# Layers: the second pair of q/k products of a half visit moved between the output turns and the output product

## The reference

```
def attn_layer(x, Wqkv, qs, ksc, Wo):
    q, k, v = split(x @ Wqkv, 3)                   # 16 heads of 64
    q = l2norm(q) * qs
    k = l2norm(k) * ksc
    q = q * cos * scale + rotate_half(q) * sin * scale
    k = k * cos / scale + rotate_half(k) * sin / scale
    out = local_attention(q, k, v)                 # windows of 32, softmax
    return out @ Wo
for i in range(6):
    x = attn_layer(shift_tokens(x), ...) + x
    x = ffn_layer(shift_tokens(x), ...) + x
```

## Time and profile before

| | us |
|---|---|
| median of 3 runs | 4645.14 (4640.55 to 4652.28) |
| profiled execution, own time | 4643.52 |
| its span, first to last instruction | 4641.7 |
| TensorE busy | 4093.0 (88%) |
| VectorE busy | 3365.0 (72%) |
| ScalarE busy | 2392.2 (52%) |
| GpSimd busy | 2163.8 (47%) |

### The profile page before, as it was taken

One profiled execution on the slowest core, in us unless ns is written; L12 is line 12 of the kernel. 1 busy time (PEld: TensorE's weight loads), 2 busy tenths in 40 slices (PEclk: granted clock), 3 DMA queues, 4 the chain that ended last, 5 costly groups with the idle time before them and its releaser, 6 DMA issues. The chain is left out here.

```text
span 4641.7 us, 175927 instructions
## 1 busy us (share of the span) xinstructions
PE 4093.0 (88%) x68914; PEld 2806.2 (60%) x68915; DVE 3365.0 (72%) x7216; ACT 2392.2 (52%) x5386; POOL 2163.8 (47%) x2301
## 2 busy tenths in 40 slices
PE   7999749576999889998899989999889998899995
PEld 4566416454666656666566665666656666566663
DVE  4777450576888778887788877888778887788876
ACT  4666423123666546665366653666536665366651
POOL 2444300103566436664366643666436664366651
PEclk9999769798999999999999999999999999999998
DMA  1000003003333223332233322333223332223221
GB/s 41 5 5 3 1 21 98 8 0 85 66 71 66 47 65 70 66 68 49 65 70 64 71 48 65 67 67 69 50 65 66 68 68 51 64 64 71 62 57 43
DMA packets 478517, 249.52 MB, mean 54 GB/s; under 512 B 65782, under 2 KB 472516, under 8 KB 476740
## 3 DMA queue, kind: packets, MB, share of 16 engines
q1 hardware_dynamic: 477764, 238.93, 23.1%
HBM read 35.40 MB, written 4.19 MB: 9 GB/s over the span
## 5 line engine op out<-in xcount | busy, mean ns | idle before, releaser
L1921 POOL TENSOR_TENSOR n_pre<-n_tt 128x512 f32<-128x512 f32 x768 | 970.9, 1275 | 886.1 <-DVE n_tt L2394 886.1
L2394 DVE TENSOR_TENSOR n_tt<-n_pp,n_rot 128x1024 f32<-128x1024 f32 x768 | 922.2, 1220 | 378.6 <-ACT n_sq L2255 378.5
L1942 POOL TENSOR_TENSOR n_pre<-n_pre,n_rn 128x512 f32<-128x512 f32 x768 | 776.6, 1042 | 284.4 <-ACT n_rn L2263 284.4
L2021 PE MATMUL n_pp<-n_wqkv,n_xT 128*128 128x512 f32 x1536 | 787.9, 615 | 10.7 <-ACT n_xT L2250 10.4
L2255 ACT ACTIVATE n_sq<-n_pp 128x512 f32<-128x512 f32 x768 | 459.1, 598 | 595.5 <-PE n_pp L2021 584.7
L2401 DVE TENSOR_REDUCE n_ss<-n_sq 128x8 f32<-128x512 f32 x768 | 518.8, 676 | 0.0
L2275 ACT COPY n_qkT<-n_pp 128x512 f32<-128x512 f32 x768 | 436.6, 594 | 136.6 <-PE n_pp L2037 136.1
L2037 PE MATMUL n_pp<-ident,n_pre 128*128 128x128 f32 x3072 | 433.2, 274 | 19.7 <-POOL n_pre L1942 14.5
L2051 PE MATMUL n_pp<-n_wo,n_OT 128*128 128x128 f32 x3072 | 398.7, 283 | 58.1 <-ACT n_OT L2281 57.1
L2037 PEld LDWEIGHTS n_pp<-ident,n_pre 128*128 128x128 f32 x3072 | 360.3, 142 | 129.1 <-issue 125.4
L2051 PEld LDWEIGHTS n_pp<-n_wo,n_OT 128*128 128x128 f32 x3072 | 361.4, 193 | 103.6 <-ACT n_OT L2281 101.2
(11 more groups left out here) (246 smaller groups left out, 7016.9 us busy)
## 6 DMA issues: line engine op xcount, KB each, us to landing
n_V<-n_Vn SPq DMA_DIRECT2D x768, 128.0 KB, 2.6
n_Vx<-n_Vn SPq DMA_DIRECT2D x384, 128.0 KB, 2.5
n_Vx<-n_Vn SPq DMA_DIRECT2D x576, 64.0 KB, 2.2
n_wqkv<-in_L_ffn_Wqkv SPq DMA_DIRECT2D x6, 1536.0 KB, 6.7
e_w<-in_L_ffn_w SPq DMA_DIRECT2D x32, 256.0 KB, 3.0
n_fxs<-X SPq DMA_DIRECT2D x48, 127.0 KB
m_Y<-e_ye SPq DMA_DIRECT2D x64, 64.0 KB, 2.1
n_wo<-in_L_ffn_Wo SPq DMA_DIRECT2D x6, 512.0 KB, 7.3
```

Source lines behind the costliest of these rows:

```text
L1921: nc.gpsimd.tensor_tensor(d, s[0], s[1][:, :, ::-1, :], ALU.add).then_inc(s_add, 1)
L1942: nc.gpsimd.tensor_tensor(d, d, bcast(rn[:, j, t, 8 * half:8 * half + 8], 2, D), ALU.mult).then_inc(s_kn, 1)
L2021: nc.tensor.matmul(pp[:, c % 2, :], xT[:, j * P:(j + 1) * P], wqkv[:, t * I + 512 * half:t * I + 512 * half + 512], start=True, stop=True) ...
L2394: nc.vector.tensor_tensor(tt[:, c % 4, :, :].rearrange("p s (h d) -> p s h d", d=D), bcast(pp[:, c % 2, :].rearrange("p (h d) -> p h d", d ...
```

## The change

In each half visit the second pair of q/k products (c = 4j+2 and 4j+3) is issued between the output turns and the output product; before, one stood behind the second turn of q/k and the other at the end of the half. The two first turns of q/k now stand together, ahead of the turns of the weights. On ScalarE the two squares follow the copies of the output and stand ahead of the exponentials. On VectorE the two rotations follow the maxima and the sum of squares 4j+1, ahead of the sums of the exponentials; the addition of the output product to X comes behind these sums, and the two sums of squares come last. `sq` has four buffers in place of two, and a square waits for the sum four before it, in place of two.

```
--- before.py
+++ after.py
@@ -1717,7 +1717,7 @@
         eye = sb("eye", [P, P], BF16)
         xs = sb("xs", [P, 2, NT, C])
         xT = sb("xT", [P, T + 1])
-        sq = sb("sq", [P, 2, 512])
+        sq = sb("sq", [P, 4, 512])
         tt = sb("tt", [P, 4, 2, 512])
         ss = sb("ss", [P, NT, 2, H])
         rn = sb("rn", [P, NT, 2, H])
@@ -2155,23 +2155,21 @@
                     elif prev:
                         turn_output(N - 1, 2, bank("o", 2, -1))
                         turn_output(N - 1, 3, bank("o", 3, -1))
+                    if nxt:
+                        project_qk(N + 1, 4 * j + 2)
+                        project_qk(N + 1, 4 * j + 3)
                     if prev:
                         output(N - 1, j, bank("y", j, -1))
                     d = j
                     if nxt or not d:
                         turn_qk(N + d, 4 - 4 * j, bank("turn", 4 - 4 * j, d))
+                        turn_qk(N + d, 5 - 4 * j, bank("turn", 5 - 4 * j, d))
                     turn_weights(N, j)
-                    if nxt or not d:
-                        turn_qk(N + d, 5 - 4 * j, bank("turn", 5 - 4 * j, d))
-                    if nxt:
-                        project_qk(N + 1, 4 * j + 2)
                     if nxt or not d:
                         turn_qk(N + d, 6 - 4 * j, bank("turn", 6 - 4 * j, d))
                         turn_qk(N + d, 7 - 4 * j, bank("turn", 7 - 4 * j, d))
                     if j == 1 and nxt2:
                         turn_x(N + 2, u, bank("x", 0, 2))
-                    if nxt:
-                        project_qk(N + 1, 4 * j + 3)
                 if not nxt:
                     weights_ready(pairs[0], N, u, 1)
                     held(pe, s_held)
@@ -2250,9 +2248,9 @@
                 nc.scalar.copy(xT[64:P, 1:T + 1], pp[64:P, bank, 0:T]).then_inc(s_xT, 1)
 
             def square(N, c):
-                after(act, s_ss, 8 * N + c - 1)
+                after(act, s_ss, 8 * N + c - 3)
                 after(act, s_qk, 8 * N + c + 1)
-                nc.scalar.activation(sq[:, c % 2, :], pp[:, c % 2, :], ACT.Square).then_inc(s_sq, 1)
+                nc.scalar.activation(sq[:, c % 4, :], pp[:, c % 2, :], ACT.Square).then_inc(s_sq, 1)
 
             def inverse_norms(N, j):
 
@@ -2326,21 +2324,19 @@
                     elif prev:
                         copy_output(N - 1, 2, bank("o", 2, -1))
                         copy_output(N - 1, 3, bank("o", 3, -1))
+                    if nxt:
+                        square(N + 1, 4 * j + 2)
+                        square(N + 1, 4 * j + 3)
                     exps(N, j, 0)
                     exps(N, j, 1)
                     if nxt or not j:
                         copy_qk(N + j, 4 - 4 * j, bank("turn", 4 - 4 * j, j))
+                        copy_qk(N + j, 5 - 4 * j, bank("turn", 5 - 4 * j, j))
                     copy_weights(N, j, 0)
                     copy_weights(N, j, 1)
                     if nxt or not j:
-                        copy_qk(N + j, 5 - 4 * j, bank("turn", 5 - 4 * j, j))
-                    if nxt:
-                        square(N + 1, 4 * j + 2)
-                    if nxt or not j:
                         copy_qk(N + j, 6 - 4 * j, bank("turn", 6 - 4 * j, j))
                         copy_qk(N + j, 7 - 4 * j, bank("turn", 7 - 4 * j, j))
-                    if nxt:
-                        square(N + 1, 4 * j + 3)
                 if nxt2:
                     copy_x(N + 2, bank("x", 0, 2))
                 if not nxt:
@@ -2399,7 +2395,7 @@
                 j, t, half = place(c)
                 after(dve, s_rn, 2 * N + j - 1)
                 nc.vector.tensor_reduce(ss[:, j, t, 8 * half:8 * half + 8],
-                                        sq[:, c % 2, :].rearrange("p (h d) -> p h d", d=D), AX.X, ALU.add
+                                        sq[:, c % 4, :].rearrange("p (h d) -> p h d", d=D), AX.X, ALU.add
                                         ).then_inc(s_ss, 1)
 
             def maxima(N, j):
@@ -2456,13 +2452,14 @@
                     maxima(N, j)
                     if nxt:
                         sum_squares(N + 1, 4 * j + 1)
+                        rotate(N + 1, 4 * j + 2)
+                        rotate(N + 1, 4 * j + 3)
+                    sum_exps(N, j)
                     if prev:
                         add_attention(N - 1, b - 1, j, at["y", j, -1][0])
-                    sum_exps(N, j)
                     if nxt:
-                        for c in (4 * j + 2, 4 * j + 3):
-                            rotate(N + 1, c)
-                            sum_squares(N + 1, c)
+                        sum_squares(N + 1, 4 * j + 2)
+                        sum_squares(N + 1, 4 * j + 3)
                     if not nxt and not j:
                         stats(layer[0] * NG, 0)
                         normalise(layer[0] * NG, 0)
```

2 lines of the change are left out of this document (removed).

## The result

| | before | changed |
|---|---|---|
| median, us | 4647.47 (4640.55 to 4652.28, 4 runs) | 5092.31 (5077.87 to 5098.34, 4 runs) |
| profiled execution, us | 4643.52 | 5092.21 |
| mean granted clock of TensorE | 0.961 | 0.944 |
| TensorE busy, us | 4093.0 (88%) | 4189.6 (82%) |

The ratio is 1.0954, 95% interval 1.0926 to 1.0981: slower by 9.5%. The forecast was 5065, range 4930 to 5175.

A forecast was written before the change was run, and what follows sets the result against it. TensorE was taken to set the pace, standing still for VectorE's late addition. On the profiled 4643.5 us, 328 for the stalls gave 4971, and 94 for the clock gave 5065; range 4930 to 5175.

The forecast's parts named there:

- The bank: TensorE's second turn of q/k waits for its PSUM bank until VectorE's late addition to X: 2.4 us per half.
- T+7.3: Predicted end of VectorE's addition with its signal, 7.3 us after the half's output turns start (T); turn due at T+4.92.
- The stall per element: Masks come 2.0 and 1.9 us later in the two halves: 3.9 us per element, 84 elements, 328 us.
- ScalarE's late exponentials: Exponentials behind the squares run 1.3 us later on ScalarE; claimed free, as VectorE reaches their sums later still.
- From masks to output turns: Program unchanged in this stretch; priced at nothing, staying 6.98 us where the clock is 1.00.
- The first and last elements: Per layer, the first can gain 13 us in all, the last lose 9.4; between these bounds nothing was taken.
- the bound of 13: Most the first elements could gain: their 2.17 us wait for the exponentials, once a layer, 13 us.
- The clock: TensorE's clock falls to half behind some stalls, costing 2.8 us per element: 84 x 0.4 x 2.8 = 94 us.
- Two in five: Share of the new TensorE stalls followed by half clock, taken from 5 of 12 similar waits in the trace.
- The Trainium skill's rule: Cycling PSUM banks with short TensorE idle times swings the clock between half and full; in full, it gives 5206.
- the rival that took it in full: Every stall is followed by the half clock: 235 us, 5206; chance 0.14, shared with more than three in five.
- that term from minus 40 to nothing: TensorE's 40.1 us of instruction waits in the product with V could vanish while it stands: 4931 at the lowest.

The follow-up runs named there:

- e1: The changed kernel with VectorE's addition of the output product to X moved between the two rotations: 4656.98 us, ratio 1.0022 to before.
- e4: The changed kernel with the addition to X also behind VectorE's two sums of squares: 5396.40 us, ratio 1.1604.
- e6: The changed kernel with the exponentials ahead of the two squares again on ScalarE: 5256.64 us, ratio 1.1311.
- e2: The changed kernel with the turns of the weights again between the first two turns of q/k, addition still late: 4908.38 us, ratio 1.0566.
- e10: As e9, but second q/k product behind the second turn of q/k, and turns of the weights between the first two turns: 4580.71 us, ratio 0.9868.
- e9: Kernel before with only product 4j+2 moved early, 4j+3 behind the last q/k turn, first two turns together, addition ahead of rotation 4j+2: 4543.25 us, ratio 0.9789.
- e3: The changed kernel with the edits of both e1 and e2: 4685.82 us, ratio 1.0087.
- e7: e1 with TensorE's two bursts of small matmuls (product with V, scores) cut in halves, large products between: 4686.53 us, ratio 1.0075.
- e8: The kernel before with the same cut of the two bursts as e7 and nothing else: 4738.45 us, ratio 1.0192.

## Why the prediction was right

**The bank.** The wait that cost nothing in the earlier trace rows is the one that decides. It was predicted at T+7.3 and came at T+7.14: the reciprocal lets the addition follow after 0.17, not after its whole 0.25, and the addition took 0.23, not 0.29. e1 takes that wait away, but for 0.2 us, and all but 10 us of the loss go with it; e4 and e6 lengthen it and the loss grows with it.

**The stall per element.** A clean half of the changed kernel takes 16.51 us, one with the turn of x 17.31 (from one second turn of q/k to the next); before, 14.59 and 15.43. That is 3.8 us per element, predicted 3.9: 84 x 3.8 = 319 us, predicted 328.

**What was priced at nothing.** ScalarE's late exponentials cost nothing, as said (e1, e6). From masks to output turns a clean half takes 7.00 against 6.98, as said. The first and last elements do not show in sum: the wait for the exponentials fell from 17.5 to 5.1 us, near the bound of 13, and small waits of the masks and of the turns grew by about as much.

**The clock.** Two in five was predicted, 60 of 168 were counted (36%). A drop cost 1.5 and 1.3 us, 2.8 in an element of two halves, as predicted, so 60 drops cost some 85 us; the term was 94. (The lost matmul time rose by more, 107 us: 1.7 a drop, of which 1.5 and 1.3 show in the time.) e2, whose 1.3 us stalls have one drop behind them in 168, gives that lost time back. That the share came out is in part luck. It was taken from twelve waits of two kinds, none of six and five of six, and nothing in them said which kind the new stall would be like; at 2.79 us (e6) it was already 98 of 168. The Trainium skill's rule ("TensorE: Matmul & The Clock Gate", section on psum-queue depth-cycling) that such idle times make the clock swing agrees with the trace for a good third of the stalls, and for 128 of 168 in e4; the rival that took it in full, 5206, was too high.

**What the sum left out.** The waits for instructions in the product with V went from 40.1 to 81.9 us. I had taken that term from minus 40 to nothing, so it had the wrong sign. 319 + 85 + 42 = 446, against the 449 us between the profiled executions. The forecast added 328 + 94 = 422: its two terms were each 9 us too large, and the 42 us were missing. So the 27 us between forecast and result are the missing term less two errors that went the other way.

## What to carry to other kernels

Where buffers are dealt out in turn, look at which engine frees each, and where that release stands in that engine's own order: a small instruction (0.2 us here) that frees a shared bank belongs ahead of long work that nobody waits for. An engine with time to spare can still set the pace, if its instruction that others wait for is queued late. After covering a wait on the busiest engine, read its other waits again, those in front of weight loads too: e1 covered one and got nothing for it, as TensorE waited as long elsewhere. With one product moved and the addition ahead of the rotations e10 gained 1.3%, and e9, with the last product ahead of the turn of x as well, 2.1%. No run separates which of e10's differences from e1 gave its gain.

## What was not expected of the hardware

- The same stall, with the same work in the 4 us before it, is followed by the half clock at one time and not at another: 60 of 168 at 2.11 us, 98 of 168 at 2.79 (e6), 128 of 168 at 3.29 (e4). What lies further back goes with it in the change: a drop followed 41 of the 63 stalls that had a wait for instructions (product with V or scores) since the stall before, and 19 of 103 that had none. In e6 it was 32 of 47 against 66 of 121, in e4 36 of 46 against 92 of 122. It does not decide alone, as both stalls shown above had such a wait, of 1.28 and 1.39 us.
- TensorE's waits for instructions stand in the product with V, 128 matmuls with their weight loads in 1.5 us, and change with what stands around it: 40 us before, 82 to 93 in the change and e1 to e3, 53 and 71 in e4 and e6, 63 and 71 in e9 and e10, and 8 with the burst cut in two (e7). In the changed kernel they occur in 51 of 106 halves without a drop of the clock and in 6 of 57 with one, so a slow TensorE rarely runs dry. What sets them was not settled.
- A half with four more changes between matmuls of 64 x 32 and of 128 x 128 tiles took 0.73 us longer without a recorded wait (e7; e8 0.72). That the changes are the cause is not shown by itself.
